# Attention on one Trainium2 core: the values matmuls of a head group run one group later, with two buffers of turned probabilities

## What is computed

```python
qkv = hidden_states @ Wqkv
q, k, v = jnp.split(qkv, 3, axis=-1)
q = rmsnorm(q, q_norm_w)
k = rmsnorm(k, k_norm_w)
...
scores = jnp.einsum('bqhd,bkhd->bhqk', q, k) * scale
scores = jnp.where(mask[None, None, :, :], scores, jnp.float32(-jnp.inf))
probs = jax.nn.softmax(scores, axis=-1)
o = jnp.einsum('bhqk,bkhd->bqhd', probs, v).reshape(b, s, h)
return o @ Wo
...
x = _layernorm(x + _L0_attn_ref(x, ...), axis=-1)
```

## Time and profile before

| | us |
|---|---|
| median of 3 runs | 1134.67 |
| lowest and highest | 1134.11, 1134.91 |
| the profiled execution's own time | 1130.08 |
| its span, first to last instruction | 1128.2 |
| granted TensorE clock, mean | 0.965 |

### The profile page before, as it was taken

The page is one execution under the profiler, slowest core; times in us unless marked ns, Lnnn a source line. Parts: engine busy times, 40 slices in busy tenths (PEclk is TensorE's granted clock), DMA queues, the critical chain, the costliest instruction groups (busy, mean ns, idle before and its releaser), DMA issues.

```text
span 1128.2 us, 19960 instructions
## 1 busy us (share of the span) xinstructions
PE 1054.4 (93%) x7180; PEld 874.4 (78%) x7180; DVE 767.7 (68%) x1173; ACT 632.9 (56%) x1287; POOL 412.1 (37%) x546
## 2 busy tenths in 40 slices
PE   4899999999999859998999999999999999999964
PEld 3677777777777648887888888888888888888853
DVE  4888787787777742593767676776867677773434
ACT  4566666666666633233565666666666666653333
POOL 4577887787777620001000010010001001004783
PEclk8899999999999996899899999999999999999988
DMA  5111111111111014135777898887888888856993
GB/s 198 42 39 31 31 31 37 53 31 31 31 31 49 20 30 139 38 122 186 225 255 241 258 280 291 256 266 260 261 263 262 289 270 260 266 170 162 234 185 110
DMA packets 125760, 175.80 MB, mean 156 GB/s; under 512 B 10624, under 2 KB 64256, under 8 KB 125664
## 3 DMA queue, kind: packets, MB, share of 16 engines
q1 hardware_dynamic: 117936, 155.92, 44.2%
q0 software_dynamic: 7728, 18.62, 7.0%
HBM read 155.90 MB, written 18.61 MB: 155 GB/s over the span
## 4 chain that ended last, share of the span: by engine, by line
PE 57%; DVE 2%; issue 1%; DMA 1%; ACT 0%; SPq 0%; POOL 0%; POOLq 0%; DVEq 0%; ACTq 0%
PE gate_ps L1299 4%; PE gate_ps L1300 3%; PE gate_ps L1301 3%; PE up_ps L1300 3%; PE up_ps L1301 3%; PE up_ps L1299 3%; PE down_ps L1326 3%; PE down_ps L1325 3%; PE down_ps L1324 3%; PE e_up_ps L1350 3%; PE e_up_ps L1351 2%; PE e_up_ps L1352 2%; PE e_gate_ps L1359 2%; PE e_up_ps L1359 2%; PE e_up_ps L1361 2%; PE e_gate_ps L1361 2%
## 5 line engine op out<-in xcount | busy, mean ns | idle before, releaser
L886 POOL DMA_INDIRECT rows<-x_dram,token_i x39 | 40.4, 1036 | 519.8 <-PE e_gate_ps L1341 424.0
L1182 DVE TENSOR_TENSOR e_lo<-e_raw,e_hi 128x1408 fp32r<-128x1408 f32 x78 | 126.5, 1623 | 45.8 <-ACT e_hi L955 45.8
L955 ACT CAST e_hi<-e_raw 128x1408 fp32r<-128x1408 f32 x78 | 107.5, 1379 | 55.8 <-PE e_up_ps L1361 55.8
L316 ACT ACTIVATE prob<-score_ps,nbias 128x256 f32<-128x256 f32 x256 | 119.8, 478 | 8.7 <-DVE nbias L412 8.6
L256 POOL TENSOR_TENSOR probT<-probT,masks 128x256 f32<-128x256 f32 x128 | 97.4, 782 | 67.1 <-DVE probT L433 67.0
L1187 DVE TENSOR_TENSOR ed_lo<-ed_raw,ed_hi 128x1024 fp32r<-128x1024 f32 x39 | 47.8, 1225 | 70.4 <-ACT ed_hi L963 70.4
L412 DVE TENSOR_REDUCE nbias<-score_ps 128x2 f32<-128x512 f32 x128 | 88.4, 691 | 4.4
L1299 PE MATMUL gate_ps<-x_hi,gu_lo 128*128 128x512 f32 x176 | 73.7, 419 | 18.0 <-issue 11.8
L324 ACT COPY probT<-probT_ps 128x512 f32<-128x512 f32 x64 | 37.6, 587 | 92.9 <-PE probT_ps L540 92.9
L506 PE MATMUL proj_ps<-wqkv_lo,xT_hi 128*128 128x512 f32 x180 | 79.4, 441 | 0.0
L904 POOL DMA_INDIRECT x1T<-expert_rows,slot_i x32 | 52.5, 1639 | 55.8 <-DMA expert_rows<-rows 45.2
(11 more groups left out here) (221 smaller groups left out, 2982.9 us busy)
## 6 DMA issues: line engine op xcount, KB each, us to landing
e_raw<-in_We_gu SPq DMA_DIRECT2D x78, 704.0 KB, 4.6
ed_raw<-in_We_down SPq DMA_DIRECT2D x39, 512.0 KB, 4.1
raw_ring<-in_Ws_gu SPq DMA_DIRECT2D x58, 256.0 KB, 5.5
wd_raw<-in_Ws_down SPq DMA_DIRECT2D x44, 256.0 KB, 5.0
expert_rows<-rows SPq DMA_DIRECT2D x39, 256.0 KB, 2.1
gu_raw<-in_Ws_gu SPq DMA_DIRECT2D x30, 256.0 KB, 5.0
ed_raw<-in_We_down SPq DMA_DIRECT2D x39, 192.0 KB, 4.7
xT_in<-in_xT SPq DMA_DIRECT2D x16, 256.0 KB, 2.8
```

Source lines behind the costliest of these rows:

```text
L316: nc.scalar.activation(prob[:, g % 2, h, :], score_ps[:, h, 0:2 * P], ACT.Exp, bias=nbias[:, s % 2, head:head + 1], scale=1.0, accum_out=r ...
L955: nc.scalar.copy(e_hi[:, half * HK:(half + 1) * HK, :], raw_half(i, half)).then_inc(e_hi_made, 1)
L1182: nc.vector.tensor_tensor(e_lo[:, part, :], raw_half(i, half), e_hi[:, part, :].bitcast(FP32), ALU.subtract).then_inc(e_lo_made, 1)
```

## The change

V of a group is issued one step later, straight behind T instead of at the end of the step: `values(n)` behind P2 becomes `values(n - 1)` between T and P1. `probT` gets a second buffer (`n % 2`), so the waits of its three writers go from `pv_mm` n to n - 1, and the two copies lose their wait on `own_made`. Since the last V of a block now comes in step g = 1 behind T, the three operations on `oT` move too: on DVE `oT` goes from ahead of the first maximum of g = 1 to behind the second, directly ahead of `oT_lo`; on ACT `oT_hi` goes from ahead of `probT_out` of g = 1 to behind the second pair of exponentials. A table of constants gets nine more columns, which nothing reads.

```diff
-        probT = sb("probT", [P, 4, 3, P])
+        probT = sb("probT", [P, 2, 4, 3, P])
...
                     wait(pool, copied, n + 1)
-                    wait(pool, pv_mm, n)
+                    wait(pool, pv_mm, n - 1)
...
                 wait(act, probT_mm, 2 * n + 2)
-                wait(act, pv_mm, n)
-                wait(act, own_made, 2 * n)
-                nc.scalar.copy(probT[:, 2:4, 0:2, :], probT_ps[1][:, 0, :].rearrange("p (h w t) -> p h w t", h=2, w=2)).then_inc(probT_act, 1)
+                wait(act, pv_mm, n - 1)
+                nc.scalar.copy(probT[:, n % 2, 2:4, 0:2, :], probT_ps[1][:, 0, :].rearrange("p (h w t) -> p h w t", h=2, w=2)).then_inc(probT_act, 1)
...
-                if g == 1 and has(s - 1):
-                    wait(act, oT_made, s)
-                    nc.scalar.copy(oT_hi[:, :, :], tiled(oT[:, :])).then_inc(oT_hi_made, 1)
                 if has(n // 4):
                     probT_out(n)
...
                 if has(s):
                     exps(s, g, 1)
+                if g == 1 and has(s - 1):
+                    wait(act, oT_made, s)
+                    nc.scalar.copy(oT_hi[:, :, :], tiled(oT[:, :])).then_inc(oT_hi_made, 1)
...
                 turned_taken(s if g else s - 1, (g - 1) % 4)
                 if behind:
                     prob_transposes(n)
+                if has((n - 1) // 4):
+                    values(n - 1)
...
-                if behind:
-                    values(n)
```

More of the change, by code:

```diff
@@ L43 @@
 C_STEP = C_TOKEN + NB
-CONST_COLS = C_STEP + TILES
+C_JOIN = C_STEP + TILES
+CONST_COLS = C_JOIN + NR
 def pieces(c, Ws_gu, Ws_down, We_gu, We_down):
@@ L253, in own_part @@
                     wait(pool, copied, n + 1)
-                    wait(pool, pv_mm, n)
+                    wait(pool, pv_mm, n - 1)
                     heads = slice(2 * pair, 2 * pair + 2)
-                    nc.gpsimd.tensor_tensor(probT[:, heads, 2, :], probT[:, heads, 0, :], own_T.unsqueeze(1).to_broadcast([P, 2, P]), ALU.mult).then_inc(own_made, 1)
+                    nc.gpsimd.tensor_tensor(probT[:, n % 2, heads, 2, :], probT[:, n % 2, heads, 0, :], own_T.unsqueeze(1).to_broadcast([P, 2, P]), ALU.mult).then_inc(own_made, 1)
             def v_difference(s):
@@ L430, in probT_out @@
                 wait(dve, probT_mm, 2 * n + 1)
-                wait(dve, pv_mm, n)
-                wait(dve, own_made, 2 * n)
-                nc.vector.tensor_copy(probT[:, 0:2, 0:2, :], probT_ps[0][:, 0, :].rearrange("p (h w t) -> p h w t", h=2, w=2)).then_inc(probT_dve, 1)
+                wait(dve, pv_mm, n - 1)
+                nc.vector.tensor_copy(probT[:, n % 2, 0:2, 0:2, :], probT_ps[0][:, 0, :].rearrange("p (h w t) -> p h w t", h=2, w=2)).then_inc(probT_dve, 1)
             split_xT(0)
@@ L447, in _ @@
                     nc.vector.tensor_copy(spread[:, :].rearrange("p (h d) -> p h d", d=HD), rinv[:, :].unsqueeze(2).to_broadcast([P, NH, HD])).then_inc(rinv_spread, 1)
[L448 to L451, removed]
                 if has(s):
@@ L459, in _ @@
                     split_wo(g)
+                if g == 1 and has(s - 1):
+                    wait(dve, pv_mm, 4 * s)
+                    wait(dve, rrep_made, s)
+                    nc.vector.tensor_tensor(oT[:, :], oT_ps[:, 0, :], oT[:, :], ALU.mult).then_inc(oT_made, 1)
                 if g == 1 and has(s - 1):
@@ L556, in values @@
                         last = nc.tensor.matmul(oT_ps[HD * h:HD * h + HD, 0, g * P:(g + 1) * P], v[:, head * HD:(head + 1) * HD],
-                                                probT[:, h, w, :], start=(w == 0), stop=(w == WB - 1))
+                                                probT[:, n % 2, h, w, :], start=(w == 0), stop=(w == WB - 1))
                 last.then_inc(pv_mm, 1)
@@ L649, in constants @@
     tables[:, C_STEP:C_STEP + TILES] = np.arange(TILES)[None, :] * P
+    tables[:, C_JOIN:C_JOIN + NR] = lane[:, None] % (P // KT) == np.arange(NR)[None, :]
     return trig, tables, masks
```

## The result

The changed kernel takes **1153.14 us** (median of 5 runs, 1152.09 to 1156.42), the kernel before 1134.11 in the runs beside it: a ratio of 1.018, interval 1.016 to 1.020. It is slower by 19.0 us; 23.3 were forecast.

A forecast was written before the change was run, and what follows sets the result against it. The prediction took TensorE's own work to bound the kernel. The 55 steps, with stall, drain and k's-square wait less the POOL wait, gave +25.3 us, the ends -2: +23.3 on 1134.67, so 1158.0 us, range 1145 to 1165.

The forecast's parts named there:

- What bounds the kernel: Middle of the attention: TensorE's own work sets the pace; V's wait for POOL's `own_part` costs 14 x 0.49 us.
- The stall of 0.26 in every step: Between U and the next S: ACT needs 2.19 us, TensorE has 1.93 us of work, so it waits 0.26.
- The drain of 0.17 between T and V: An extra change of tile shape behind T delays the next piece by 0.17 us a step, 9.4 us over 55.
- Rival 1: The stall is there but the drain is hidden under weight loads: +13.9 us, 1148.6 us; chance 0.13.
- rivals 3 and 4: 3: ACT keeps up, only the drain costs, +0.5, chance 0.07. 4: ACT keeps up, no drain, -8.8, chance 0.07.
- rival 5: DVE, late from g = 1, also delays U or the norm: +30 us and above, 1165 us; chance 0.06.
- The term of oT, oT_hi and oT_lo: P1 of g = 2 waits for k's square, delayed by the moved `oT` operations: 0.6 us once a block.
- rival 2: Stall and drain are there, the wait for k's square is not: +14.9 us, 1149.5 us; chance 0.15.
- The two ends: Block 0 and the end of the attention: V behind T fills some waits, -2 us, bounds 0 and -7.4.
- The sum: Whole kernel: +25.3 us for the 55 steps and -2 for the ends give +23.3 us, 1158.0 us.

The follow-up runs named there:

- The last experiment: Kernel before, with the second pair's half of `own_part` at g = 1 made by DVE instead of POOL: 1125.86 us, ratio 0.993.
- the pair with the extra copy: One added 512-column ACT copy per step behind the copy of U's result: in the kernel before 1132.37 us, in the changed kernel 1189.54 us.
- the kernel with the last block put back: Changed kernel, with block 15's V at the end of its own step and its `oT_hi` ahead of `x1`'s copy again: 1150.02 us.
- the run with the extra copy: Changed kernel with one added 512-column ACT copy directly ahead of `oT_hi`, once a block at g = 1: 1169.75 us, ratio 1.032.

## Why the prediction was right, point by point

**What bounds the kernel** was right: TensorE's own work and one wait worth 14 x 0.49 us. The last experiment took away that wait and left V where it was: it gained 6.6 us in the medians and 6.0 in the middle of the profile, of the 6.9.

**The stall of 0.26 in every step** was right, and is shown by three runs: the pair with the extra copy (0 us and 36 us) and the exponentials put first for g < 3 (steps of 5.97). One step in four the profile names no exponential, since `kT_lo` from the same copy comes late as well. S was only drawn wrongly: it starts at once and waits inside, for the exponentials of its last heads.

**The drain of 0.17 between T and V** was right to a hundredth. T to V was forecast at 1.02 and is 1.03 and 1.02 in the rows above; T to P1 is 0.85 as soon as V stands elsewhere. An unstalled step is 5.97 us with four borders and 5.78 with three. By this the trace agrees with the Trainium skill's page TensorEngine Tiling (Key Properties), which says that a change of tiling mode drains TensorE. Rival 1 is out by it, rivals 3 and 4 by the steps of 6.24, and rival 5 by the time.

**The term of oT, oT_hi and oT_lo was mis-sized**, and it is the largest error: TensorE was to wait 0.6 us at P1 of g = 2 and waits about 0.1, which over 14 blocks is the 7 us between +25.3 and +18.3. Its path was as described. From S of g = 1 (235.10), with 0.25 for the stall inside S, `oT_hi` was forecast at 241.40 and starts at 241.44, and `oT_lo` follows 0.65 later. But it takes 0.69 and not 1.18. The prediction had both ends and chose 1.18 "since POOL is busy". What mattered was not how busy POOL is but which of the two starts first: in before, `oT_lo` (at 252.22) began 0.11 behind a POOL operation, in after 0.15 ahead of one. In the middle rival 2, which left this wait out, is nearly the truth: 55 x 6.22 - 325.25 = 16.9. Its time, 1149.5, is also nearer to the measured 1153.14 than the forecast's 1158.0: the prediction had the right mechanism with this one term of it too large.

**The two ends were mis-sized.** -2 was taken of a range from 0 to -7.4; the profiled executions show +1.1 and +5.2, outside it. Of the 5.2 only some 1.5 are the change's order, the rest is the clock of that execution. The middle takes the same time wherever it runs the same code (343.53 and 343.47 us in after and in the kernel with the last block put back), so the medians leave 19.0 - 18.3 = 0.7 us for all that lies outside it; this is an estimate, and too small to settle the sign. No -2 is seen either way. The waits of V for POOL are gone in this profile as said. But the bounds were drawn from what could be won alone; the prediction named that the last V has no later step and gave it no price. Nor did it follow `oT_hi` at the end, which moved behind `x1`'s copy. At the start, in block 0, S waits 1.31 us for the exponentials:

```profile
45.04 1.14 PE L526 MATMUL score_ps<-kT_lo,qT_hi 32*128 32x384 f32 x2 [1.31 <-ACT prob L317]
```

**The sum**, 23.3 against 19.0 in the medians and 26.2 in the profiled spans, was helped by two errors of opposite signs: 7.0 too much in the middle, and outside it some 3 too little by the medians, 10 too little by the profiled spans (+1.1, +5.2 and +1.6 in the feed-forward part, where -2 was forecast). That the medians came within 4.3 us is in part luck. In which stretch the executions without a trace are shorter can't be read.

## What to carry to other kernels

Before work is moved off a wait, ask what it covered where it stood: here 0.79 us of V hid a path through ScalarE that had 0.53 us of slack, and 0.5 us of wait once a block was traded for 0.26 in every step and a further border of tile shapes. A wait may be the last link of a full chain on another engine; then changing the order moves it (V of g = 2, U of g = 3), and only a shorter chain removes it. The first and last blocks, where the next step's work is missing or waits itself, need a count of their own, with losses in it, and one profiled execution is not enough to measure them where the clock changes in them.

## What the runs showed of the hardware

VectorE and GpSimd did not merely slow each other when both ran instructions with two operands in SBUF: in each place looked at, the one that started later stood still until the other had ended. `oT_lo`, 0.69 us where it led, ended 0.56 behind POOL's addition in the run with the extra copy (250.98 + 1.27 = 252.25; 251.36 + 1.45 = 252.81). In after it led, ended at 242.78, and POOL's addition, 1.27 where it led, ended 1.14 behind that (242.24 + 1.68 = 243.92). Both ended their own duration less 0.13 behind the other's end, as if they had begun just before it. DVE's `weigh` at 242.71, which reads PSUM, took its usual 0.68 beside the same addition. In the kernel with work taken off POOL, DVE's 0.92 us multiplication ended at 250.33, 0.29 behind a POOL multiplication of 0.74 us that had started 0.11 earlier (no run shows it without a neighbour):

```profile
249.30 0.74 POOL L258 TENSOR_TENSOR probT<-probT,masks 128x256 f32<-128x256 f32 x1
```

These rows bear out the Trainium skill's page SBUF — State Buffer (section SBUF: two separate sides), by which the port pair that the two share is an exclusive lock: whichever starts first has it for the whole instruction, and the other is fully blocked. The prediction priced this as a constant 1.18 us; it is a race, and 0.15 us of lead is worth 0.5 us here. So the half microsecond ahead of `oT_hi` could cost 1.26. No run varied the lead alone, with all else fixed.
